# Three instead of two of the state space's sixteen C products on GpSimd, and one row load issued ahead of a store

## What is computed

```python
u, z = halves of layernorm(x) @ W_in.T          # u: causal convolution of 4 taps, then silu
dt = clip(softplus(u @ low @ W_dt.T + b_dt), 0.001, 0.1)
B, C = u @ W_x.T rows for the 16 states
h[n] = exp(dt * A[n]) * h[n] + (dt * u) * B[n]   # for each of 16 states n, along time
y = sum over n of h[n] * C[n]
y = (y + u * D_param) * silu(z)
out = y @ W_out.T + residual
```

## Time and profile before

| | us |
|---|---|
| median of 3 runs (lowest, highest) | 3924.9 (3922.84, 3928.5) |
| the profiled execution's own time | 3911.12 |
| its span | 3908.8 |
| busy in the span: PE, DVE | 3396.3 (87%), 2898.4 (74%) |
| busy in the span: ACT, POOL | 1905.3 (49%), 1548.9 (40%) |
| state space scans, first start to last end | 2054.2 to about 2973.4 |

### The profile page before, as it was taken

How to read it: one execution, slowest core, us unless ns; L and a number is a source line. 1 busy time by engine, 2 the same in 40 slices (tenths; PEclk the granted TensorE clock), 3 DMA queues, 4 the chain that set the end, 5 groups by cost and what they waited for, 6 DMA issues and landing times. The chain is left out here.

```text
span 3908.8 us, 60860 instructions
## 1 busy us (share of the span) xinstructions
PE 3396.3 (87%) x21111; PEld 2086.5 (53%) x21164; DVE 2898.4 (74%) x6458; ACT 1905.3 (49%) x3463; POOL 1548.9 (40%) x1015
## 2 busy tenths in 40 slices
PE   5999999887999997587758898888886999999987
PEld 3666676555777763354423343333333666666653
DVE  7888888556777767533229999999997777777765
ACT  2555555324565552222237776777773333333325
POOL 2311111452121210588848888887872011111112
PEclk9999999998999998788879999999998999999989
DMA  6333332004444424233332332222221222222211
GB/s 153 92 88 88 88 89 67 1 2 108 101 101 103 100 62 139 58 43 43 44 73 82 95 105 85 95 85 81 88 87 56 88 88 87 86 88 86 87 58 44
DMA packets 242531, 314.21 MB, mean 80 GB/s; under 512 B 46450, under 2 KB 157779, under 8 KB 231588
## 3 DMA queue, kind: packets, MB, share of 16 engines
q1 hardware_dynamic: 208308, 289.02, 26.4%
q0 software_dynamic: 22528, 17.32, 3.2%
q10 hardware_dynamic: 11392, 3.97, 0.5%
HBM read 251.93 MB, written 57.08 MB: 79 GB/s over the span
## 5 line engine op out<-in xcount | busy, mean ns | idle before, releaser
L574 DVE TENSOR_REDUCE a_Mx<-a_Sx 128x2 f32<-128x512 f32 (+1 forms) x1024 | 590.5, 618 | 173.0 <-PE a_Sx L626 127.2
L2215 POOL TENSOR_TENSOR a_inp<-a_dtu,a_Bs 128x1024 f32<-128x1024 f32 x256 | 597.4, 2360 | 50.0 <-DMA a_Bs<-a_brows 42.5
L2493 DVE TENSOR_TENSOR_SCAN a_h<-a_dA,a_inp 128x1024 f32<-128x1024 f32 x256 | 581.5, 2282 | 21.6 <-ACT a_dA L2376 17.1
L2621 PE MATMUL a_Y<-a_hc,g_ident 128*128 128x512 f32 x1024 | 486.6, 603 | 4.1 <-DVE a_hc L2505 3.4
L347 POOL TENSOR_TENSOR a_rest<-a_qk,a_parts 128x512 f32<-128x512 f32 x64 | 75.1, 1173 | 916.8 <-ACT a_parts L399 916.8
L2376 ACT ACTIVATE a_dA<-a_dtA,a_A 128x512 f32<-128x512 f32 x512 | 330.9, 681 | 141.0 <-DVE a_h L2493 140.1
L413 ACT ACTIVATE a_Pr<-a_SA 128x512 f32<-128x512 f32 x512 | 305.3, 596 | 167.4 <-DVE a_SA L524 79.2
L623 PE MATMUL a_Sx<-att_Kp,att_Qp 96*128 96x256 bf16 (+1 forms) x2048 | 346.1, 261 | 41.2 <-DMA att_Qp<-a_crows 18.3
L1962 ACT ACTIVATE f_sg<-f_GB 128x512 f32<-128x512 f32 x272 | 162.5, 598 | 435.6 <-PE f_GB L2038 435.4
L2088 PEld LDWEIGHTS f_OUT<-g_routed_wd,f_hm 128*128 128x128 f32 x2176 | 280.6, 191 | 124.5 <-issue 90.5
L2621 PEld LDWEIGHTS a_Y<-a_hc,g_ident 128*128 128x128 f32 x1024 | 196.3, 193 | 216.1 <-issue 213.5
(11 more groups left out here) (482 smaller groups left out, 6934.3 us busy)
## 6 DMA issues: line engine op xcount, KB each, us to landing
a_Bs<-a_brows SPq DMA_DIRECT2D x256, 256.0 KB, 3.2
f_Cs<-f_crows SPq DMA_DIRECT2D x512, 128.0 KB, 2.8
att_Qp<-a_packing SPq DMA_DIRECT2D x192, 192.0 KB
att_Kp<-a_packing SPq DMA_DIRECT2D x192, 192.0 KB
a_packing<-a_parts SPq DMA_DIRECT2D x64, 384.0 KB, 2.8
a_packing<-a_parts SPq DMA_DIRECT2D x64, 128.0 KB, 2.8
a_Cs<-a_brows SPq DMA_DIRECT2D x32, 256.0 KB, 4.8
g_x<-x SPq DMA_DIRECT2D x8, 512.0 KB, 7.3
```

Source lines behind the costliest of these rows:

```text
L574: nc.vector.tensor_reduce(Mx[(k + 2 - (j < LATE)) % 2][:, t, 2 * jj:2 * jj + 2], Sx[t][:, 0:2 * wd].rearrange("p (h q) -> p h q", h=2), AX ...
L2215: nc.gpsimd.tensor_tensor(inp[n % Q][:], dtu[k][:], Bs[n % Q][:].unsqueeze(1).to_broadcast([P, CH, GT]), ALU.mult).then_inc(s["mulB"], 1)
L2493: nc.vector.tensor_tensor_scan(h[n % 2][:].rearrange("p c q -> p (c q)"), dA[m % 2][:].rearrange("p c q -> p (c q)"), inp[n % Q][:].rearra ...
L2621: nc.tensor.matmul(Y[c][:], ident[:], hc[i % Q][:, c], start=(i == 0), stop=(i == N - 1))\
```

## The change

`MOVED` becomes (2, 5, 8): the product of state 8 goes from DVE to POOL, with a third tile for a C row and a third load of it in each group. PE no longer spreads C[8], and its sum 8 waits for POOL's product. In the SP loop the load of B row 14, in step 11, is issued ahead of the store of `bf` instead of behind it. (The lines of load and store become L2178 and L2182.)

```diff
-        MOVED = (2, 5)
+        MOVED = (2, 5, 8)
...
                 for n in range(N):
-                    if on(1) and n == 11:
-                        wait(sp, s["m_read"], U * (g + 1) + BF_AT)
-                        sp.dma_start(brows[(k + 1) % 2], bf[0:2 * N, :]).then_inc(s["b_out"], 16)
                     if on(0) if n < N - 3 else on(1):
                         if n == N - 3:
                             wait(sp, s["b_out"], 16 * (g + 2))
...
                             .then_inc(b_in[nn % Q], 16)
+                    if on(1) and n == 11:
+                        wait(sp, s["m_read"], U * (g + 1) + BF_AT)
+                        sp.dma_start(brows[(k + 1) % 2], bf[0:2 * N, :]).then_inc(s["b_out"], 16)
```

## The result

The changed kernel takes 3915.3 us, the kernel before 3924.7 us in the same comparison: ratio 0.9976, 95% interval 0.9969 to 0.9983. That is 9.4 us less, 0.24% (7 to 12 us by the interval); the forecast was 8.8 less.

A forecast was written before the change was run, and what follows sets the result against it. The bound was taken as a ring from DVE's product 3 through PE and ACT back to DVE; 1.28 + 14 x 0.44 + 1.34 = 8.8, so 3924.9 - 8.8 = 3916.1, range 3905 to 3924.

The forecast's parts named there:

- The ring: Steady groups: DVE's product 3 releases CC(4), PE works to wbc, ACT to decay 14, DVE from scan 14 onward; 57.73 a group.
- The steady group, 0.44: Groups 1 to 14: of 1.34 freed, 0.88 goes into scan 9's wait for decay 9, leaving 0.44 a group.
- Two limits: Steady group at CC(11): product 10 gives about 2437.10, PE's own list 2437.09, so 0.44 was taken.
- Groups 0 and 15: First and last group: nearly all of the 1.34 passes, 1.28 in group 0 and 1.34 in group 15.
- SP's order: Load of row 14 ahead of the store: GpSimd's 2.75 wait goes, but off the path, so worth nothing.
- Sum: Whole kernel: 1.28 + 14 x 0.44 + 1.34 = 8.8 less, giving 3916.1.
- 1.7 of cover: Product 8 on GpSimd ends at 2431.77, scan 10 needing it is due at 2433.44: 1.7 to spare.
- The rival that they exclude each other: GpSimd and DVE: each moved product pushes a scan by 2.35, 16 slower, 3941; chance 0.02.
- A: All groups: DVE is the bound and all 1.34 passes, 21.4 less, 3903.5, period 56.4; chance 0.12.
- B: Steady groups swallow the gain, only groups 0 and 15 gain, 2.6 less, 3922.3, period 57.7; chance 0.15.

The follow-up runs named there:

- either cut alone: The changed kernel with PE adding only 32 of 512 columns of state 7 (ratio 0.9975), or with Identity for u's silu (0.9974).
- both cuts: The changed kernel with most of state 7's sum left out and Identity for u's silu: 3909.3 beside 3925.2, ratio 0.996.
- early product 0: MOVED = (0, 2, 5) in place of the change's (2, 5, 8), PE's sums in old order, GpSimd making product 0 right behind scan 0: 3909.4 beside 3923.0, ratio 0.9969.
- the first attempt to free the ring: The changed kernel with PE's sums 6 to 12 moved in its list and u's silu put behind decay 9: 3959.2 beside 3925.2, ratio 1.0092.

## Why the prediction was right

**The ring.** Right. Only what shortens the ring, from DVE's scan 0 to product 3 and over PE and ACT to the next group, counted: product 0, in DVE's part of it, passed 1.28 of 1.34; product 8, inside the stretch where PE is full, 0.45; product 1, where GpSimd had no cover, cost 0.37.

**The steady group, 0.44.** Measured 57.73 - 57.28 = 0.45. Scan 9 was to wait 0.88 for decay 9 and waited 0.77. The difference is only in how idle time is counted, from scan 8's end (2.28 behind its start) and not from where a merged scan would start (2.18): scan 9 starts 2443.85 - 2440.80 = 3.05 behind scan 8, forecast 3.06. PE's side came out as worked out too, with wbc at the place that the list without CC(8) gives it and no wait in between.

**Two limits.** Right in kind: either cut alone gained nothing, both together gained. Wrong in what lies behind them. The full 1.34 doesn't come free, since product 9 waits for CC(9) next (0.59) and the period stops at 56.90. The prediction named no third limit there. Its size can be worked out. Where product 9 waits for CC(9), it starts 0.41 behind the start of CC(9) (2442.61 to 2443.02 without the silu). In the changed kernel the row of CC(9) on PE starts at 2445.44, so product 9, which starts at 2446.23, could start at 2445.85 and no earlier: 0.38, just what both cuts gave.

**Groups 0 and 15.** The working gave 1.28 for group 0. From scan 0 of group 0 to scan 0 of group 1 it was 56.11 before and is 55.24: 0.87 gained. The rest, 0.4, went at scan 4. It waited 1.07 for GpSimd before, and now, 14.43 after the first scan instead of 13.91:

```profile
2085.75 2.29 DVE L2493 TENSOR_TENSOR_SCAN a_h<-a_dA,a_inp 128x1024 f32<-128x1024 f32 x1 [1.59 <-ACT a_dA L2376]
```

By the rows the cause is PE's clock and not the moved product. PE had stood still 11.4 us ahead of its first CC in both. Behind that the clock stayed lower for longer in the changed kernel. PE there:

```profile
2075.39 3.62 PE L2621 MATMUL a_Y<-a_hc,g_ident 128*128 128x512 f32 x4
2078.80 1.06 PE L2556 MATMUL a_M<-g_ident,a_xn 128*128 128x128 f32 x4
```

and in the kernel before:

```profile
2058.32 3.02 PE L2621 MATMUL a_Y<-a_hc,g_ident 128*128 128x512 f32 x4
2061.18 0.60 PE L2556 MATMUL a_M<-g_ident,a_xn 128*128 128x128 f32 x4
```

The granted clock was 0.50 from 2075 to 2079, and 0.59 from 2057.9 to 2061.2 in the kernel before. The layer norm's transposes came later and took 1.06 instead of 0.60, and with them ACT's list, decay 4 in it. The three other kernels with the changed kernel's steps 0 to 5 in group 0 (the change without SP's order, the one with sum 7 left out, the one without silu) show the same again: 3.62, 1.06, scan 4 at 14.43 and 55.24. The kernel with both cuts has product 8 too, but its passes took 3.47 and its transposes 0.60, its scan 4 waited 1.08 for GpSimd, and its group 0 took 54.87, a gain of 1.24, near the 1.28 (its two edits act in group 0 as well). So the term was mis-sized by 0.4: it had no place for PE's clock, and PE's list up to that point is the same in all of these. For groups 14 and 15 together 0.44 + 1.34 = 1.78 was forecast; they give 57.73 - 57.65 = 0.08 and 54.21 - 52.51 = 1.70, again 1.78. What scan 0 of group 15 lost, group 15 got back; why it was late is open. So the forecast 8.8 holds within 0.3 for the stage because thirteen groups gave 0.45 as worked out, while group 0's 0.4 is a real miss that is small beside them.

**Sum.** From the stage's first scan to the first addition to x of its last group it is 2974.56 - 2054.25 = 920.3 before and 2983.10 - 2071.32 = 911.8 now: 8.5 less where 8.8 was worked out. The medians say 9.4, with 7 to 12 as the interval; the last us is not told apart.

**GpSimd.** Right: 1.7 of cover foretold, 1.7 measured; 2.38 for the product. **SP's order.** Right: worth nothing, by its own run, with the wait gone. **GpSimd and DVE side by side.** The rival that they exclude each other is out. The scans take what they took:

```profile
L2493 DVE TENSOR_TENSOR_SCAN a_h<-a_dA,a_inp x256: 2262/2283/2292, 2071.3 to 2979.6; 128x1024 f32<-128x1024 f32 x128
```

with three products in each group on GpSimd, and four products made the kernel faster still. The Trainium skill's warning (Perfetto Trace Analysis, Optimizing Scalar/DVE Operations) that moving work between the two might not help isn't borne out for these operations.

**The rivals A and B.** That all 1.34 passes (period 56.4) and that nothing does (57.7) were both excluded by the period. A's full 1.34 is nearly reached in another place: product 0 passes 1.28 of it.

## What to carry to other kernels

When the engine that looks busiest is relieved, ask where in each turn of the loop its list meets another engine's full stretch: one more product moved away gave 1.28, 0.45 or -0.37 a group, by its place in the ring and the cover that GpSimd had there, and even the best place cost 0.3 until the lists of PE and GpSimd were put in an order that suited it. Find out whether several limits meet there before one is removed, since removing one of two gives nothing. And after a reordering look at every read that an in-order engine stands at: what is queued behind it may be the next thing on the path.

## What the runs showed of the hardware

Behind a pause of PE of 2.80 us (and of 11.4 us in group 0) the granted clock was 0.50, and four passes took 3.62 instead of 1.88. Behind pauses of 1.17, 1.09 and 2.10, in the kernel with an early product 0, they ran at full rate. But behind one of 1.97, in the first attempt to free the ring, they took 1.88 in two steady groups and 2.9 to 3.6 in the others, so the length of the last pause doesn't decide it by itself. A pause of PE that costs nothing by itself can be paid for in slow passes, where these lie on the path. In the kernel before it happens behind the pause ahead of CC(1) in six of the fourteen steady groups, and is hidden there, since the period is 57.73 with it and without:

```profile
2405.08 0.39 PE L2588 MATMUL a_CC<-a_bc,g_state_sel 128*128 128x512 bf16 x1 [2.51 <-DVE a_hc L2505]
2405.31 3.57 PE L2621 MATMUL a_Y<-a_hc,g_ident 128*128 128x512 f32 x4
```

How much of the passes behind it is slow differed between executions with the same list up to there: in group 0, behind 11.4 us of pause in each, the four passes took 3.02, 3.47 and 3.62 us (kernel before, with both cuts, changed); and from group to group, as in the kernel before, where the four passes behind the same pause of 2.51 took anything from 1.88 to 3.57.
